# Layer norm applied on GpSimd instead of ScalarE, and GpSimd's operands exchanged

## The reference

```
x = x + 0.5 * ffn(layernorm(x), w_gate, w_up, w_down)
x = x + ssm(layernorm(x), W_z, W_params, conv_w, W_dt, b_dt, A_log, D, W_out)
x = x + 0.5 * ffn(layernorm(x), w_gate, w_up, w_down)

layernorm(x) = (x - mean(x)) / sqrt(var(x) + 1e-5)     # over the 256 channels
ffn(x)       = (silu(x @ Wg.T) * (x @ Wu.T)) @ Wd.T    # 768 hidden channels
```

## Time and profile before

| | |
|---|---|
| time, median of 3 runs | 2368.41 us (2367.46 to 2369.61) |
| span of the profiled execution | 2367.9 us |
| VectorE busy | 2230.9 us, 94% |
| TensorE busy | 2177.0 us, 92% |
| GpSimd busy | 2079.4 us, 88% |
| ScalarE busy | 1984.1 us, 84% |
| transfers | 291.21 MB, 123 GB/s mean |

### The profile page before, as it was taken

The page is one execution under the profiler, slowest core; times in us unless marked ns, Lnnn a source line. Parts: engine busy times, 40 slices in busy tenths (PEclk is TensorE's granted clock), DMA queues, the critical chain, the costliest instruction groups (busy, mean ns, idle before and its releaser), DMA issues. The chain is left out here.

```text
span 2367.9 us, 28924 instructions
## 1 busy us (share of the span) xinstructions
PE 2177.0 (92%) x9220; PEld 1344.3 (57%) x9220; DVE 2230.9 (94%) x2456; ACT 1984.1 (84%) x2876; POOL 2079.4 (88%) x1382
## 2 busy tenths in 40 slices
PE   7986999999999999999999999999999999999578
PEld 4452656556565656656565665655556565565346
DVE  2599999999999999999999999999999999999993
ACT  5988888897988889798888979888898988988672
POOL 2588989999998999999999999999999899999773
PEclk9997999999999999999999999999999999999799
DMA  2122334433343443434343334433434344333221
GB/s 88 37 76 68 141 126 135 142 137 141 128 142 133 137 140 126 146 132 142 134 135 143 126 134 138 148 134 135 142 126 143 132 139 140 135 125 122 71 67 37
DMA packets 112027, 291.21 MB, mean 123 GB/s; under 512 B 11201, under 2 KB 45314, under 8 KB 111874
## 3 DMA queue, kind: packets, MB, share of 16 engines
q1 hardware_dynamic: 111874, 289.35, 35.6%
HBM read 271.49 MB, written 17.83 MB: 122 GB/s over the span
## 5 line engine op out<-in xcount | busy, mean ns | idle before, releaser
L1104 POOL TENSOR_TENSOR acc<-acc,ring 128x1024 f32<-128x1024 f32 x512 | 1209.2, 2362 | 86.1 <-DVE ring L1302 70.8
L1266 DVE TENSOR_TENSOR_SCAN g_bank<-du_bank,ring 128x1024 f32<-128x1024 f32 (+1 forms) x512 | 1098.7, 2152 | 3.2 <-ACT ring L1026 0.2
L778 PE MATMUL work<-wd_t,hid 128*128 128x256 f32 x3072 | 678.9, 380 | 8.8 <-DVE hid L1219 7.9
L1302 DVE SCALAR_TENSOR_TENSOR ring<-g_bank,inv_a,ring 128x1024 f32<-128x1024 f32 (+1 forms) x576 | 662.9, 1156 | 10.5 <-POOL acc L1104 2.7
L778 PEld LDWEIGHTS work<-wd_t,hid 128*128 128x128 f32 x3072 | 583.2, 190 | 106.0 <-issue 14.8
L1026 ACT ACTIVATE ring<-dt,a_coef 128x1024 f32<-128x1024 f32 (+1 forms) x576 | 575.1, 1046 | 24.3 <-DVE g_bank L1266 23.3
L845 ACT ACT_TABLE_LOAD x271 | 347.7, 1283 | 4.8
L909 ACT ACTIVATE sil<-work 128x512 f32<-128x512 f32 x384 | 222.3, 597 | 119.6 <-PE work L766 118.7
L766 PE MATMUL work<-xt_hi,wg_t 128*128 128x512 f16 x768 | 294.0, 383 | 22.0 <-ACT sil L909 7.1
L766 PE MATMUL work<-xt_hi,wu_t 128*128 128x512 f16 x768 | 294.2, 383 | 21.6 <-ACT sil L909 7.5
L1072 POOL TENSOR_TENSOR hid<-hid,sil 128x512 f32<-128x512 f32 x192 | 244.1, 1274 | 65.5 <-ACT hid L917 43.0
(11 more groups left out here) (98 smaller groups left out, 2761.1 us busy)
## 6 DMA issues: line engine op xcount, KB each, us to landing
ring<-c_rows SPq DMA_DIRECT2D x448, 512.0 KB, 3.6
ring<-c_rows SPq DMA_DIRECT2D x64, 256.0 KB, 3.2
x_in<-L_attn_x SPq DMA_DIRECT2D x30, 512.0 KB, 4.0
out<-x_fin SPq DMA_DIRECT2D x30, 512.0 KB, 4.8
x_fin<-L_attn_x SPq DMA_DIRECT2D x2, 512.0 KB, 5.8
c_rows<-params SPq DMA_DIRECT2D x32, 32.0 KB, 3.3
out<-x_in SPq DMA_DIRECT2D x2, 512.0 KB, 2.9
ring<-L_ffn_w_gate SPq DMA_DIRECT2D x1, 768.0 KB, 5.8
```

What stands on the lines that cost most here:

```text
L778: last = pe.matmul(dst[:, j * E:(j + 1) * E], hid[:, K.unit[f, bt, c, m] % HIDS, t:t + P], wd_t[:, m, :], start=(m == 0), stop=(m == HM - 1))
L1104: nc.gpsimd.tensor_tensor(v, v, shaped(bt, cg[:, K.number[ev[1:]] % TERMS, :]), ALU.add).then_inc(S["summed"], 1)
L1266: scan = nc.vector.tensor_tensor_scan(g, du_h, d_h, first[0], ALU.add, ALU.mult)
L1302: nc.vector.scalar_tensor_tensor(v, g, inv_a[:, h, s:s + 1], c_row, ALU.mult, ALU.mult).then_inc(S["weighted"], 1)
```

## The change

GpSimd executes the norm: one tensor_scalar for each row of 256, which subtracts the mean and multiplies by the reciprocal deviation, with both as per-partition operands. ScalarE has no norm any more. The negated mean (VectorE), the shift (GpSimd) and the tile shift are gone. In `schedule` the norm is placed at least 0.002 units behind its reciprocal deviation, since both are now GpSimd's. In five of GpSimd's instructions, `hp`, `rp`, `ra`, `gate` and `cm`, the two operands trade places: the tile that is overwritten was the first operand and becomes the second. The softplus and the differences of u stay as they are, and so do the tables.

```diff
@@ -377,7 +377,11 @@
         for name, ev in row_events(b):
             table = own if name in own else ROW
             i = seen[name] = seen.get(name, -1) + 1
-            out.append((round(SLOTS * b + table[name][i], 3), len(out), ev))
+            at = table[name][i]
+            if ev[0] == "lx":
+                rstd = "lr" + name[2:]
+                at = max(at, (own if rstd in own else ROW)[rstd][i] + 0.002)
+            out.append((round(SLOTS * b + at, 3), len(out), ev))
...
@@ -471,9 +475,9 @@
         if kind == "sj":
             return [("stats", 1)]
         if kind == "ln":
-            return [("meanvar", 1), ("turned", 1)]
+            return [("meanvar", 1)]
         if kind == "lr":
-            return [("rstd", 2), ("shift", 1)]
+            return [("rstd", 2)]
...
@@ -515,7 +519,6 @@
         rstd = sb("rstd", [P, 2, TJ])
-        shift = sb("shift", [P, 2, TJ])
...
@@ -847,18 +850,7 @@
             for ev in K.order:
                 kind = ev[0]
-                if kind == "lx":
-                    _, f, bt, c = ev
-                    slot = K.at["normed", ev][1] % 2
-                    src = {1: x_of(bt), 2: x_mid[bt % 2], 3: fin(bt)}[f]
-
-                    wait(act, "shift", ("lr",) + ev[1:])
-                    wait(act, "ready", K.was[ev])
-                    for j in range(TJ):
-                        last = nc.scalar.activation(normed[slot][:, j, :], src[:, c * TJ + j, :], ACT.Identity,
-                                                    bias=shift[:, slot, j:j + 1], scale=rstd[:, slot, j:j + 1])
-                    last.then_inc(S["normed"], 1)
-                elif kind == "Te":
+                if kind == "Te":
...
@@ -1038,7 +1030,7 @@
                 kind = ev[0]
                 if kind == "lr":
                     _, f, bt, c = ev
-                    slot = K.at["shift", ev][1] % 2
+                    slot = K.at["meanvar", ("ln",) + ev[1:]][1] % 2
...
@@ -1048,9 +1040,17 @@
                     nc.gpsimd.tensor_tensor(r, meanvar[:, slot, :, 1], eps[:], ALU.add).then_inc(S["rstd"], 1)
                     wait(pool, "rstd", ev, less=1)
                     nc.gpsimd.tensor_tensor(r, r, minus_half[:], ALU.pow).then_inc(S["rstd"], 1)
-                    wait(pool, "rstd", ev)
-                    wait(pool, "turned", ("ln",) + ev[1:])
-                    nc.gpsimd.tensor_tensor(shift[:, slot, :], shift[:, slot, :], r, ALU.mult).then_inc(S["shift"], 1)
+                elif kind == "lx":
+                    _, f, bt, c = ev
+                    slot = K.at["normed", ev][1] % 2
+                    src = {1: x_of(bt), 2: x_mid[bt % 2], 3: fin(bt)}[f]
+                    wait(pool, "rstd", ("lr",) + ev[1:])
+                    wait(pool, "ready", K.was[ev])
+                    for j in range(TJ):
+                        last = nc.gpsimd.tensor_scalar(normed[slot][:, j, :], src[:, c * TJ + j, :],
+                                                       meanvar[:, slot, j, 0:1], rstd[:, slot, j:j + 1],
+                                                       ALU.subtract, ALU.mult)
+                    last.then_inc(S["normed"], 1)
...
                     k = K.at["silu", ("si",) + ev[1:]][1] % SILUS
-                    nc.gpsimd.tensor_tensor(v, v, sil[:, k, :], ALU.mult).then_inc(S["product"], 1)
+                    nc.gpsimd.tensor_tensor(v, sil[:, k, :], v, ALU.mult).then_inc(S["product"], 1)
...
                     v = x_mid[bt % 2][:, t, :].rearrange("p j e -> p (j e)")
-                    nc.gpsimd.tensor_tensor(v, v, x_of(bt)[:, t, :].rearrange("p j e -> p (j e)"),
+                    nc.gpsimd.tensor_tensor(v, x_of(bt)[:, t, :].rearrange("p j e -> p (j e)"), v,
                                             ALU.add).then_inc(S["mid_added"], 1)
...
                     v = fin(bt)[:, t, :].rearrange("p j e -> p (j e)")
-                    nc.gpsimd.tensor_tensor(v, v, x_mid[bt % 2][:, t, :].rearrange("p j e -> p (j e)"),
+                    nc.gpsimd.tensor_tensor(v, x_mid[bt % 2][:, t, :].rearrange("p j e -> p (j e)"), v,
                                             ALU.add).then_inc(S["fin_added"], 1)
...
                     v = part(bt, p, acc[bt % 2])
-                    nc.gpsimd.tensor_tensor(v, v, part(bt, p, zs), ALU.mult).then_inc(S["gated"], 1)
+                    nc.gpsimd.tensor_tensor(v, part(bt, p, zs), v, ALU.mult).then_inc(S["gated"], 1)
...
                     v = part(bt, p, acc[bt % 2])
-                    nc.gpsimd.tensor_tensor(v, v, shaped(bt, cg[:, K.number[ev[1:]] % TERMS, :]),
+                    nc.gpsimd.tensor_tensor(v, shaped(bt, cg[:, K.number[ev[1:]] % TERMS, :]), v,
                                             ALU.add).then_inc(S["summed"], 1)
...
@@ -1181,9 +1181,6 @@
                     for j in range(TJ):
                         last = nc.vector.bn_aggr(meanvar[:, slot, j, :], stats[:, slot, j, :])
                     last.then_inc(S["meanvar"], 1)
-                    wait(dve, "meanvar", ev)
-                    nc.vector.tensor_scalar(shift[:, slot, :], meanvar[:, slot, :, 0], -1.0, None,
-                                            ALU.mult).then_inc(S["turned"], 1)
```

## The result

The changed kernel takes 2947.38 us (median of three runs, 2946.97 to 2948.03) against 2368.41 us: a ratio of 1.2442, interval 1.2425 to 1.2459. It is slower by 579 us, and the prediction had 2319 us, faster. The profiled execution spans 2945.6 us.

A forecast was written before the change was run, and what follows sets the result against it. VectorE was taken to pace the body at 99%. Of the 61.4 us leaving it a fifth was given back: 2367.9 - 0.8 x 61.4 = 2318.8, plus 0.5: 2319 us, range 2302 to 2440 (likeliest case alone 2302 to 2337).

The forecast's parts named there:

- What bounds the kernel: VectorE paces the body (120 to 2250 us), busy 2105.11 of 2130 us, 99%; GpSimd is second.
- VectorE's 61.4 us: Negated mean leaves VectorE: 58.4 us busy, held by GpSimd instructions, plus 3.0 us idle; a fifth of the gain given back.
- case D: TensorE cannot follow VectorE: half of the gain, 2337 us; inside the forecast's own range, sharing its 0.60.
- GpSimd's operands: In GpSimd's five sums and products, the overwritten tile as second operand makes them cheaper: 244 us gained in the body.
- The Trainium skill's rule on two operands: GpSimd's two operands share one read port, floor 2.1 to 2.2 ns a column; by it the swap gives 0 us.
- The norm's price: One GpSimd norm instruction of 256 columns costs 0.49 us, bounds 0.31 and 0.73: +172 us in the body.
- Case C: Swap works but GpSimd's norm is dearer, 1.02 us an instruction: 2365 us, about nothing; chance 0.10.
- New waits: GpSimd's block of sum, power and norm takes 3.4 us, covered by VectorE's slack of two buffers; TensorE waits for normed.
- rival B: Operand swap does nothing, GpSimd paces with a body of 2184 us instead of 2130: 2422 us; chance 0.30.

The follow-up runs named there:

- trailing lines: 22 GpSimd test instructions added at the very end of the kernel before, on tiles nobody needs, to read their durations; the whole run about 30 us longer.
- run with early place and cheap operands: Changed kernel with the norm directly behind its reciprocal deviation and GpSimd's five sums and products' second operand starting one column later: 2559.61 us (1.0798).

## Why the prediction was wrong, point by point

- **What bounds the kernel.** Right: VectorE paced the body, and taking its negated mean away made the kernel faster (2336.76 us).
- **VectorE's 61.4 us.** The reading of the held time is borne out: of the 96 negated means in the kernel before 59 took more than 0.25 us, and each of these ended within 0.06 us of the end of a GpSimd instruction. The term was mis-sized where it was given back: with the norm still on ScalarE 32 us arrived, about half, as in case D (2337 us), and not four fifths. In the changed kernel itself nothing of it could be seen.
- **GpSimd's operands.** This step failed: 0 us, not 244. The rows left two reasons open, and the prediction leaned to the order because two offsets, 1 and 2 columns, had one price. Both are distances that the trailing lines show cheap, where 4 and 64 are dear. Two points that agree did not test the other reason; an instruction with equal starts would have.
- **The Trainium skill's rule on two operands** (GPSIMD Engine Reference, sections 2.1 and 3.1), by which the exchange would gain nothing, came out right on that. In step, from 512 to 1024 columns (1.27 to 2.36 us), a column costs 2.13 ns, which agrees with the 2.1 to 2.2 ns that the prediction worked out from it. As a floor it is not borne out: with the second input one column later (1.09 to 2.00 us) a column costs 1.78 ns. L1062, which the prediction put below the floor, lies there only by such a difference; its whole 1094 ns are 2.14 ns a column.
- **The norm's price.** This step failed too: 1.22 us, outside its bounds of 0.31 to 0.73. Neither end was a bound: the upper one took a sum of two tensors as dearer than two operations on one, and the trailing lines show the reverse, 1.27 us for 512 columns against 2.08. Case C (1.02 us) was close in size and had 0.10, but only together with a working exchange.
- **New waits.** This step failed, and it is the one that no rival held. The prediction asked whether VectorE could stand the norm's block, and named TensorE's wait without a price. The block of sum, power and norm that it put at 3.4 us takes 6.1 (0.21 + 1.03 + 4.84), and VectorE did wait for sums (219.5 us). The norm kept a place in the order that was made for ScalarE; on GpSimd it stood behind sums and products that themselves wait for ScalarE and TensorE. That place costs 255 us with all of the norm (2947 to 2692) and 215 us with a quarter of it (2582 to 2367).
- **The sum of rival B** holds once its price and the place are mended. With 1.22 us: 1965 - 25 + 429 + 72 = 2441 us of body, 311 over 2130, 2679 us; measured 2692. With half of it 2465, measured 2471. In the run with early place and cheap operands, where GpSimd is at 92% of the body, it fails (2435 against 2560).
- Together: of 579 us, 255 are the norm's place in GpSimd's queue and 325 the work of three quarters of the norm; the last quarter, the missing negated mean and ScalarE's relief cancel at 2367 us. The split depends on the order in which the two are taken: at the old place three quarters of the work are worth 365 us (2947 to 2582), and the place then 215. The exchange is 0.

## What to carry to other kernels

Before work is moved to another engine, run one instruction of it there: the nearest rows bound a different operation. Then ask of the move not only whether the new engine has time, but what stands ahead of the moved step in its queue and who waits behind it; a step that was ready early on one queue can be the last on another, and with a quarter of the work the loss was already 9%. Where two reasons explain the same rows, find the row that parts them before leaning on either.

## What the runs showed of the hardware

GpSimd's two-tensor operations on fp32 are 14% cheaper (1.09 against 1.27 us for 512 columns) when the second input starts 1 or 2 columns later than the first; at 4, 8, 16 and 64 columns, and with the first input 1 column later, they are as dear as in step. The target's position and the order by itself change nothing. The differences of u (1.90 us for 1024 columns, first input 1 column later in one tile) do not fit and are not explained. GpSimd's tensor_scalar with two operations takes 0.37 us and 3.33 ns a column, more per column than a sum of two tensors (2.13 ns in step). VectorE's small negated mean took 0.17 to 1.50 us beside GpSimd's instructions, and each of the 59 over 0.25 us ended within 0.06 us of the end of one of them.
